# Attention and experts on one core: the rounds of the attention loop written out one after the other

## The reference

```python
def attn(x):                                   # 3 heads, each 512 wide, softmax over keys, full
    Q, K, V = (einsum('bne,hde->hbnd', x, W) for W in (Wq, Wk, Wv))
    w = softmax(einsum('hbnd,hbmd->hbnm', Q, K) / sqrt(512), axis=2)
    # axis 2 of (h, b, n, m) is n
    return mean_over_heads(einsum('hbnm,hbmd->hbnd', w, V)) @ fc_w.T + fc_b

x1 = layernorm(x + attn(x))
x2 = layernorm(x1 + cross_attention(x1, ctx))  # 16 heads, 32 wide, causal mask
out = layernorm(x2 + experts(x2))              # 64 experts, top 6, at most 128 tokens each,
                                               # and one shared gated feed-forward
```

## Time and profile before

| | |
|---|---|
| median of 3 runs | 2179.55 us (2175.96 to 2187.16) |
| the profiled execution | 2161.92 us |
| its span, first to last instruction | 2160.2 us |
| its instructions | 46551 |
| mean granted TensorE clock | 0.982 |
| preparation | about 0 to 69 us |
| attention, rounds 0 and 1 | about 69 to 198 us |
| attention, the loop (rounds 2 to 15) | about 198 to 1344 us |
| attention, rounds 16 and 17 | about 1344 to 1430 us |
| experts | the rest |

### The profile page before, as it was taken

The page is one execution under the profiler, slowest core; times in us unless marked ns, Lnnn a source line. Parts: engine busy times, 40 slices in busy tenths (PEclk is TensorE's granted clock), DMA queues, the critical chain, the costliest instruction groups (busy, mean ns, idle before and its releaser), DMA issues.

```text
span 2160.2 us, 46551 instructions
## 1 busy us (share of the span) xinstructions
PE 2017.0 (93%) x16976; PEld 1238.1 (57%) x16976; DVE 1711.7 (79%) x3877; ACT 1025.5 (47%) x1569; POOL 733.1 (34%) x710
## 2 busy tenths in 40 slices
PE   8999998998998998998988988889999999999998
PEld 3666565665665665655655655445555555555553
DVE  5568977977977978878878879865888888888867
ACT  5434443434434434434534525444565665656645
POOL 1003313213223223223223222244455565564533
PEclk9999999999999999999999999899999999999999
DMA  6700110010010110110110112258999999999948
GB/s 234 57 23 33 31 42 30 22 52 29 23 52 15 37 52 10 42 52 10 42 52 10 42 42 97 68 144 249 280 311 292 299 293 286 305 284 313 287 105 312
DMA packets 134389, 267.77 MB, mean 124 GB/s; under 512 B 32699, under 2 KB 42939, under 8 KB 134236
## 3 DMA queue, kind: packets, MB, share of 16 engines
q1 hardware_dynamic: 110108, 226.06, 32.0%
q0 software_dynamic: 24128, 40.01, 9.5%
HBM read 208.67 MB, written 57.42 MB: 123 GB/s over the span
## 4 chain that ended last, share of the span: by engine, by line
PE 54%; DVE 24%; issue 12%; ACT 5%; POOL 3%; DMA 1%; DVEq 0%; ACTq 0%; POOLq 0%
PE moe_bank L1712 24%; PE ring L920 18%; DVE quad L1300 5%; PE moe_bank L1781 4%; DVE inv_denominator L1316 3%; POOL scratch L890 3%; PE fold L485 2%; ACT scratch L1182 2%; DVE scratch L1264 2%; DVE maxima L1300 2%; DVE scratch L1310 2%; PE moe_bank L1747 1%; PE quad L1035 1%; PE moe_bank L1759 1%; ACT scratch L1162 1%
## 5 line engine op out<-in xcount | busy, mean ns | idle before, releaser
L178 POOL DMA_INDIRECT slot_table<-table_records,slot_of_choice x204 | 202.4, 992 | 650.8 <-PE ring L920 487.5
L1162 ACT ACTIVATE scratch<-ring 128x512 f16<-128x512 f32 x224 | 131.8, 595 | 323.4 <-PE ring L920 320.7
L920 PE MATMUL ring<-xT_split,tion_then_expert_weights 128*128 128x256 f16 x2304 | 267.3, 273 | 0.0
L920 PE MATMUL ring<-tion_then_expert_weights,xT_split 128*128 128x512 f16 x1152 | 264.6, 379 | 0.0
L920 PEld LDWEIGHTS ring<-xT_split,tion_then_expert_weights 128*128 128x128 f16 x2304 | 220.5, 98 | 38.9 <-issue 10.3
L890 POOL TENSOR_SCALAR_AFFINE_SELECT scratch<-scratch 128x1024 f32<-128x1024 f32 x64 | 96.9, 1513 | 322.0 <-ACT scratch L1182 318.4
L1264 DVE SCALAR_TENSOR_TENSOR scratch<-ring,scratch 128x512 f16<-128x512 f32 x192 | 127.9, 685 | 79.0 <-ACT scratch L1162 41.5
L920 PEld LDWEIGHTS ring<-tion_then_expert_weights,xT_split 128*128 128x128 f16 x1152 | 110.3, 98 | 125.7 <-DVE scratch L1264 2.9
L1661 POOL DMA_INDIRECT expert_sums<-tion_then_expert_weights,scatter_index x64 | 117.2, 1831 | 170.0 <-DMA expert_sums<-tion_then_expert_weights,scatter_index 42.0
L1300 DVE CUSTOM_DVE_ANT_0 quad<-quad,causal_penalty 128x128 f32<-128x128 f32 (+1 forms) x512 | 165.3, 395 | 3.0 <-PE quad L1018 1.7
L980 PE MATMUL ring<-scratch,weights_split 128*128 128x512 f16 x576 | 132.0, 379 | 14.2 <-DVE weights_split L1278 14.2
(11 more groups left out here) (251 smaller groups left out, 4108.8 us busy)
## 6 DMA issues: line engine op xcount, KB each, us to landing
gate_up_landing<-in_w_gate SPq DMA_DIRECT2D x43, 704.0 KB
gate_up_landing<-in_w_up SPq DMA_DIRECT2D x43, 704.0 KB
scratch<-in_w_down SPq DMA_DIRECT2D x43, 512.0 KB
scratch<-in_w_gate SPq DMA_DIRECT2D x21, 704.0 KB
scratch<-in_w_up SPq DMA_DIRECT2D x21, 704.0 KB
tion_then_expert_weights<-in_w_down SPq DMA_DIRECT2D x21, 512.0 KB
scratch<-in_w_down SPq DMA_DIRECT2D x43, 192.0 KB
xT_in<-in_xT SPq DMA_DIRECT2D x16, 512.0 KB, 4.2
```

The lines of the kernel that those rows point to most:

```text
L178: pool.indirect_dma_start(self.dram, bass.IndirectOffsetOnAxis(ap=self.slot[:, tb, c:c + 1], axis=0), self.record[:, tb, c, :], None, boun ...
L920: last = pe.matmul(out_, left(a, c), right(b, c), start=(n == 0 and not onto), stop=(n == 3 * chunks - 1))
L1162: act.activation(half(0), src, ACT.Copy, scale=scale).then_inc(high, 1)
```

## The change

The loop over rounds 2 to 15 and the four calls around it become one Python loop over all 18 rounds. Each `Body(i)` has a number for i. On every engine this leaves out the loop's registers and its branch; the counts of all waits and the places of the transfers in DRAM are constants. The steps, their order, their buffers and their waits are the same.

```diff
     def bodies(eng, emit):
 
-        emit(Body(0))
-        emit(Body(1))
-        with eng.Fori(2, B) as i:
+        for i in range(B + 2):
             emit(Body(i))
-        emit(Body(B))
-        emit(Body(B + 1))
```

## The result

The changed kernel took 2101.68 us in the median of three runs (2088.78 to 2110.33), the kernel before 2179.55. The ratio is 0.963, with a 95% interval of 0.9541 to 0.972. The profiled execution took 2088.78 us around a span of 2087.0, 73.2 us less than the span before. The forecast was 57.7 us less, a median of 2121.9 and a range down to 2106: the right sign and the right place, and 15.5 us of gain missed between the profiled executions, 20.2 between the medians.

A forecast was written before the change was run, and what follows sets the result against it. TensorE (PE), busy 93% of the span, was taken as the bound, standing still behind VectorE's stall at each back edge. Back edges 57.7 us, registers, fetching 0: 2179.55 - 57.7 = 2121.9 us, range 2106 to 2143.

The forecast's parts named there:

- Back edges: Loop of rounds 2 to 15: removing 13 taken branches back gains 57.7 us, 4.44 each for twelve.
- the control: First round of the loop, entered without a backward branch: 77.87 us, taken as the length of rounds after the change.
- The reader of q14: Instruction queue q14, 56 packets from 300 to 1260 us: taken to be DVE's code, read again in every round.
- Fetching: Written-out rounds: PE needs 82 more code packets, at most 0.05 us a crossing, 4 us in all; taken as 0.
- The clock: PE's granted clock in the loop: stays at 1.00 once the idle 3.4 us at the seam go.
- The parts of a seam: Typical back edge: 2.8 us empty stretch of DVE, about 1.3 us K job at the lower clock, the rest lower clock.
- Registers: Sequencer steps working out DVE's waits in each round: hidden behind running instructions, so 0.
- The sign that the prediction named for this term: Register term is wrong if the first round of the loop itself becomes shorter than 77.87 us.
- The far end of that term: Register work: 26.9 us of gain if all 672 steps of 40 ns for L1218 on DVE lay open.
- The 17.6 us between the profiled execution and the median: Kernel before: median 2179.55 us is 17.6 above the profiled execution; no place known, left as they are.
- The rival that tied them to back edges: Each back edge costs more in unprofiled runs, 13 x 5.46 = 71 us gained: 2108.6 us (12%).
- The other rivals: Clock falls anyway, 2143.1 (10%); DVE stalls at new code blocks, 2176.5 (4%); PE's code comes late, 2351 (3%).

The follow-up runs named there:

- dve_head64: Kernel before, loop kept on all engines, VectorE's loop starting at the 64th instruction of a code block; usual round 77.81 us, loop 1091.2 us.
- dve_regs: Changed kernel, rounds written out, but VectorE's waits still worked out from a register, in a loop that runs once; median 2100.24 us, ratio 0.9631 to the kernel before.
- the three starts: Kernel before with VectorE's loop starting at instruction 64, 96 or 0 of a code block; loops 1091.2, 1144.3 and 1093.2 us.
- dve_looped: Rounds 2 to 15 written out for TensorE, ScalarE, GpSimd and SyncE, VectorE keeping its loop; ratio 0.9997 to the kernel before, loop 1141.8 us.
- dve_written: Rounds 2 to 15 written out for VectorE alone, the four other engines keeping their loop; median 2107.86 us, ratio 0.9675 to the kernel before.
- the holds: Changed kernel plus one VectorE reciprocal of 200, 412 or 485 columns at the start of rounds 3 to 15; loops 1087.9, 1115.0 and 1126.5 us.
- dve_regs_nolink: Written-out kernel with VectorE's register waits, but constants for the waits in its chains of small instructions; usual round 77.29 us, loop 1081.2 us.
- dve_head0: Kernel before with VectorE's loop starting at the first instruction of a code block; median 2124.79 us, ratio 0.9701 to the kernel before.
- dve_head96: Kernel before with VectorE's loop starting at instruction 96 of a code block; usual round 81.9 us, loop 1144.3 us.
- these four kernels: The kernel before, and the changed kernel with a VectorE reciprocal of 200, 412 or 485 columns added at the seam; loops 1145.9, 1087.9, 1115.0, 1126.5 us.

## Why the prediction missed

**Back edges: right in place and size.** 13 back edges were put at 57.7 us, by taking the first round of the loop as the control. dve_head64 takes away their fetch: leaving out its first round, which pays one stall at the entry (81.75 against 77.85 us), its loop would be 1087.3 us, 58.6 us below the kernel before. It is not the same sum to the letter. It also holds the gap in front of L1229, which goes (14 x 0.20 = 2.8 us, and the control round had it), while a seam with the branch in place keeps some 0.35 us (TensorE's gap in front of the K job is 0.58 us in dve_head64 and 0.23 in dve_regs, 4.6 us over 13 seams), which the control round had not. With both put right it would be some 60 us. That the stall goes with a fetch was shown by the three starts: packets and stall come and go together, with branch, registers and steps unchanged.

**The reader of q14: right.** It was argued from the stall alone. Moving DVE's code makes the packets come and go.

**Fetching: right, at nothing.** 82 packets were worked out, and 79 came in the stretch from 300 to 1260; dve_looped and dve_written show no cost of PE's. DVE does lose tenths of a microsecond near its own packets: 0.29 us, put down to issue, in one round of dve_regs, and the 0.20 of L1229. That the packet is the cause is not shown.

**The clock: right for this change.** It stayed at 1.00. The parts of a seam were less certain than written. In the kernel before a back edge cost 4.05 us in the steady rounds, the holds say 1.68 us for one fall of the clock, and 2.8 + 1.68 is more than 4.05, so the two do not simply add; how much of the lower clock is hidden at that seam stays open.

**Registers: the step that failed.** The forecast took 0, from a chain of small instructions that lasted 2.37 us with registers and without. That reading is right (dve_regs_nolink) but stood for the wrong half of the waits: each wait of the chain has an instruction of 160 ns to hide behind, those on other engines at times have none. The sign that the prediction named for this term came up: round 2 itself became shorter than 77.87. The changed kernel's round is 76.70 us and not 77.87, 1.17 us less, 15.7 to 16.4 us over 14 rounds. By the runs 9.9 us of it come with DVE's registers (dve_regs), of which 8.0 are paid in every round at the waits on other engines, and 1.3 us are the other engines' loops and registers (dve_written). Of the rest, some 5 us, the 0.20 us in front of the second L1229 make up 14 x 0.20 = 2.8: it is not in front of L1229 in dve_head64, dve_head0 and dve_head96, so it belongs to where the code lies, and the control round had it too. Some 2 us stay open. For the control round alone the account closes: round 2 of dve_regs takes 77.77 us, and the 0.10 us by which a round of dve_written exceeds one of the changed kernel make it 77.87.

**The control was not quite the changed kernel.** It lacked the branch, but had the registers and the place of the code. The step took them for nothing on the strength of one chain. The far end of that term, 26.9 us on the gaining side, was written down, and then the range stopped at 2106: from 2121.9 it would have reached 2095 and held the 2101.68. That would have been luck: the 26.9 counted the 672 steps of `link`, which turned out free, and left out DVE's other 49 steps a round, some of which were not.

**The 17.6 us between the profiled execution and the median** were left where they were. The rival that tied them to back edges (2108.6) came nearer to the median than the forecast did, but by luck. dve_looped stalls at each of its back edges like the kernel before, and its profiled span was 18.1 us longer; yet its loop was 4.1 us shorter, and all of the excess lay behind the loop (836.9 us against 816.1). What lies there varied by 35 us over the 14 executions. The executions of the kernel before that were not profiled have no trace, so for them this is an inference. The other rivals did not come true: the clock did not fall, and in the changed kernel neither DVE nor PE has idle time of microseconds at new blocks.

## What to carry to other kernels

Look behind each engine's branch, not at it: here the engine that stood still there was the one whose code was fetched again in each round, and it took another engine and its clock down with it. In this kernel the body was brought back by moving its start, or by a hint on the branch, which had about three quarters of what writing out gave (54.7 and 53.2 us of 73.4 in the loop). Check in the instruction queue that the packets are gone. When a first, unbranched round serves as the control, list what it still has in common with the loop, and price waits worked out from registers at a place where nothing runs to cover them.

## What the runs showed of the hardware

A round of 315 VectorE records, in packets of 8.2 KB, stayed at hand when it ended within three blocks of 128 and was fetched again in every round when it reached a fourth. PE kept the whole of its round, with no packet on q8 from 300 to 1260 us. The Trainium skill (Runtime: NRT & Kernel Launch, section Instruction fetch mechanics) has two blocks of 16 KiB, 256 instructions each, and a fetch where a taken branch leaves them. That one body is run again without a packet and another is fetched in each round agrees with it. The size of the blocks does not: VectorE's packets hold 8.2 KB and come singly, one for each 130 records or so, and on this the measurement decides. How much is kept the three starts do not settle. It can be three blocks of 128 records, or two of 256 if the loops began in the second half of one (128 + 64 + 315 = 507 records would fit, 128 + 96 + 315 = 539 would not).

A gap of one length at the same seam lowered TensorE's clock in some rounds and not in others, in these four kernels more often the longer it was: 0, 6, 9 and 13 of 13 for 1.34, 2.66, 3.13 and 3.4 to 3.7 us. Each fall cost 1.68 us of the round where DVE was held up (80.92 against 79.24 us, and 81.41 against 79.73).
